# A change of TensorE's order inside the context loop of a Perceiver block: one run of sixteen 256-column matmuls a tile, in chunks 1 to 16

## The chip, the cores and the metric

The kernel runs on one core of a Trainium2 chip. The metric is the device time of one execution in microseconds (us). The kernel before took 857.74 us (median of three runs, 857.46 to 857.77).

## The reference, cut to what matters

128 latent tokens attend with linear attention to 12,544 context tokens of width 512 (16 heads of 32, 64 features a head); then come a second attention of cumulative sums and a router of two experts, which the change does not touch. Of the context the block needs

```python
k = heads(key, Wk, bk, Sk)                       # context @ Wk.T + bk
v = heads(value, Wv, bv, Sk)                     # context @ Wv.T + bv
k_prime = jax.nn.relu(jnp.einsum('bhnd,fd->bhnf', k, Wkf))
k_prime = k_prime * attention_mask[:, None, :, None]
kv = jnp.einsum('bhnf,bhne->bhfe', k_prime, v)   # summed over the tokens n
k_sum = jnp.sum(k_prime, axis=2)
```

## The kernel before, in words

**Precision.** Every operand of a large product is kept as two fp32r tensors: a high part (ScalarE's copy, rounded) and a low part (the rest, by a subtraction of VectorE or GpSimd). A full product is three matmuls, low x high, high x low and high x high (`three`, L808 to L812).

**Tiling.** The context comes in chunks of 512 tokens (24 of them, 0 to 23, and a last half chunk; `LAST` is 24), a chunk in four tiles of 128 tokens. For tile `n` = 4c + t TensorE does, in `period`:
- `values(n)`: jobs 0 and 1 of the features, then the tile's values into `v_bank`, 12 matmuls of 512 columns;
- `keys(c + 1, .., t)`: a quarter of the keys of the next chunk into `k_bank`, 12 matmuls of 512 columns, with jobs 2 and 3 behind the first three;
- `key_values(n - 1)`: features times values of the tile before, 8 matmuls of 256 columns, summed in `kv_ps` over the whole context.

A feature job (`feature_job`, L883) is two matmuls of 256 columns: keys of the tile by the high and low feature weights side by side. Jobs 0 and 2 go to the bank `f_ps[0]`, 1 and 3 to `f_ps[1]`. So in a tile there are two runs of 256-column matmuls, one of twelve (`key_values` and jobs 0, 1 of the next tile) and one of four (jobs 2, 3), and 24 matmuls of 512 columns.

**The other engines, in the order of their programs, for one tile:**
- ScalarE (`tile`, L589): the low half of jobs 0 and 1 out of the bank (`features_share`, L575: into the two-slot buffer `fb`), the high part of the features of the tile before (`features_high`, L581), the values' high part (L566), the high part of a context tile (`split_ctx_high`, L550), the shares of jobs 2 and 3, the keys' high part (`keys_high`, L558, two halves).
- VectorE (`tile`, L1316): sums of jobs 0, 1 (`features_sum`, L1287: bank plus `fb`, into `kf`), `features_low` of the tile before (L1300), the values' low part (L1278), sums of jobs 2, 3, relu and mask (`masked_features`, L1294), the keys' low part (`keys_low`, L1270, two halves).
- GpSimd (`period`, L464): the low part of a context tile (`split_ctx_low`, L453), then the features added to their running sum (`add_features`, L460), which waits for `kf_ready` (the mask).
- SyncE loads half a chunk of context at a time into the single buffer `ctx_raw`, when GpSimd has taken the low part of what was in it (L375, L376).

Each engine's queue is in order; semaphores with counts tie them. Work of chunks 17 to 21 on VectorE and ScalarE holds extra pieces besides (row sums, the split of later weights); in chunks 1 to 16 there are none.

Of the kernel before, what the change touches and what calls it, by code (L numbers as in the profile page):

```python
# [4 lines left out]
P = 128  # L5
D = 512
KC = D // P
# [6 lines left out]
CHUNK = 2 * HALF  # L14
TILES = CHUNK // P
NH_CTX = S_CTX // HALF
LAST = NH_CTX // 2
LAST_TILES = NH_CTX % 2 * (HALF // P)
NT = S_CTX // P
GRP = P // HD  # L20
GF = GRP * FD
# [2 lines left out]
JOBS = 4  # L24
# [38 lines left out]
def perceiver_kernel(nc, x_in, ctx_in, mask_in, wq_in, bq_in, wk_in, bk_in, wv_in, bv_in, bdq_in, bdk_in,  # L63
                     bo_in, wo_in, wr_in, stream_in, ident_in, tri_in, out):
    f32, f32r = mybir.dt.float32, mybir.dt.float32r
    ALU, ACT, AX = mybir.AluOpType, mybir.ActivationFunctionType, mybir.AxisListType

    ctx = ExitStack()
    with ctx:
# [146 lines left out]

        k_ps, v_ps = [k_bank[:, :], v_bank[:, :]], [kv_bank[1], kv_bank[2]]
        turn_ps = [kv_bank[3], f_ps[1]]
        o_ps = [v_bank, kv_bank[1]]
        val_ps = [kv_bank[1][:, 0:D // 2], kv_bank[2][:, 0:D // 2]]  # L220
        sum_ps = [f_ps[1][:, 0:D // 2], kv_bank[0][:, 0:D // 2]]
# [45 lines left out]
        ctx_lo_ready = sem("ctx_lo_ready")  # L267
# [3 lines left out]
        k_done = sem("k_done")  # L271
        k_hi_ready = sem("k_hi_ready")
        k_lo_ready = sem("k_lo_ready")
# [165 lines left out]
        def _(pool):  # L439
# [16 lines left out]
            def add_features(n, t, first=False):  # L456
# [4 lines left out]
                                   ksum_acc[:, :].rearrange("p (j f) -> p j f", f=P), kf[:, t % 2, :, :], ALU.add)\  # L461
                    .then_inc(ksum_added, 1)

            def period(c, s, splits=TILES):  # L464

                n = TILES * c
                for t in range(TILES):
                    if t < splits:
                        split_ctx_low(n + 2 * TILES + t, s, t)
                    add_features(n + t, t)  # L470
# [8 lines left out]
            for t in range(TILES):  # L479
                split_ctx_low(2 * TILES + t, 0, t)  # L480
                add_features(t, t, first=t == 0)
            with pool.Fori(1, LAST - 3, 2) as c:
                period(c, 1)
                period(c + 1, 0)
            period(LAST - 3, 1)
# [52 lines left out]
        def _(act):  # L538
# [47 lines left out]
                js = slice(b * NPAIR // 2, (b + 1) * NPAIR // 2)  # L586
                act.activation(kf_2[:, t, js, 0, :], kf[:, t, js, :], ACT.Copy).then_inc(kf_hi_ready, 1)

            def tile(n, t, first=False, keys=(), splits=()):  # L589

                for i in range(2):
                    features_share(n, i, first and t == 0)
                if not (first and t == 0):
                    features_high(n - 1, t - 1)
                values_high(n, t, first)
                for x in splits:

                    split_ctx_high(*x)
                features_share(n, 2, False)
                features_share(n, 3, False)  # L600
                for k in keys:
                    keys_high(*k)
# [24 lines left out]
            def period(c, s, splits=TILES, keys=CHUNK, pieces=0):  # L627
                n = TILES * c
                for t in range(TILES):
                    tile(n + t, t, keys=((c + 1, 1 - s, t, k_bank, keys),),  # L630
                         splits=((2 * c + 4 + t // 2, s, t),) if t < splits else ())
                    if pieces:
                        qkv_high(TILES * (pieces - 1) + t)

# [34 lines left out]
            with act.Fori(1, LAST - 5, 2) as c:  # L669
                period(c, 1)  # L670
                period(c + 1, 0)
            act.wait_ge(early_loaded, 16 * NPIECE)
            act.wait_ge(row_sums_ready, 2 * KC)
# [133 lines left out]
        def _(pe):  # L807
# [58 lines left out]
            def values_0(jobs):  # L866
# [13 lines left out]
                feature_job(*jobs[1])  # L880
                value_step(0, 0, 0, 3)

            def feature_job(c, s, n, t, i, first=False):  # L883

                if t == 0:

                    pe.wait_ge(k_lo_ready, 2 * (KC * c + i + 1))
                if not (first and t == 0 and i < 2):

                    pe.wait_ge(fsum_ready, JOBS * n + i - 1)  # L890
                for j in (2 * i, 2 * i + 1):
                    last = pe.matmul(f_ps[i % 2][:, (j % 2) * 2 * P:(j % 2 + 1) * 2 * P],  # L892
                                     keys_2[:, s, j, t * P:(t + 1) * P], bd[:, :, :].rearrange("p x f -> p (x f)"),
                                     start=True, stop=True)
                last.then_inc(f_done, 1)
# [35 lines left out]
                    if t > 0:  # L931
                        key_values(t - 1, t + 1, first=t == 1)

            def period(c, s, n_keys=CHUNK):
                n = TILES * c
                for t in range(TILES):
                    jobs = [(c, s, n + t, t, i) for i in range(JOBS)]
                    values(n + t, s, t, jobs[0:2])
                    keys(c + 1, 1 - s, t, jobs[2:4], n_keys)
                    key_values(n + t - 1, t + 1)  # L940

# [145 lines left out]
            pe.wait_ge(bd_lo_ready, 1)  # L1087

            period_0()
            with pe.Fori(1, LAST - 3, 2) as c:  # L1090
                period(c, 1)
                period(c + 1, 0)
            period(LAST - 3, 1)
            period(LAST - 2, 0)
            period(LAST - 1, 1, HALF)
            period_last(LAST, 0)
# [145 lines left out]
        def _(dve):  # L1242
# [48 lines left out]
            def masked_features(n, t):  # L1291

                dve.wait_ge(fsum_ready, JOBS * n + JOBS)
                dve.tensor_scalar(kf[:, t % 2, :, :], kf[:, t % 2, :, :], 0.0, mask[:, bass.ds(n, 1)], ALU.max,  # L1294
                                  ALU.mult)\
                   .then_inc(kf_ready, 1)

            def features_low(n, t):
                dve.wait_ge(kf_hi_ready, n + 1)
                dve.tensor_tensor(kf_2[:, t % 2, :, 1, :], kf[:, t % 2, :, :], kf_2[:, t % 2, :, 0, :].bitcast(f32),  # L1300
                                  ALU.subtract)\
                   .then_inc(kf_lo_ready, 1)
# [13 lines left out]
            def tile(n, t, first=False, keys=()):  # L1316

                features_sum(n, t, 0, first)
                features_sum(n, t, 1, False)
                if first and t == 0:  # L1320
                    queries_out()
                else:
# [46 lines left out]
            def period(c, s, keys=CHUNK, pieces=0, sums=None):  # L1369
                n = TILES * c  # L1370
                for t in range(TILES):
                    if sums is not None:
                        row_sum(sums, t)
                    i = TILES * (pieces - 1) + t
                    if pieces and i:
                        qkv_low(i - 1)
                    tile(n + t, t, keys=((c + 1, 1 - s, t, k_bank, keys),))

            def queries_out():
                for b in range(2):  # L1380
# [46 lines left out]
            with dve.Fori(1, LAST - 7, 2) as c:  # L1427
                period(c, 1)
                period(c + 1, 0)
            dve.wait_ge(sums_loaded, 16 * 2)  # L1430
            for i in range(2):
                period(LAST - 7 + i, 1 - i, sums=i)
# [220 lines left out]
```

## Time and profile before

| | |
|---|---|
| median of three runs | 857.74 us |
| the profiled execution | 857.43 us |
| its span | 855.5 us |
| TensorE, matmuls | 848.3 us busy, 99% of the span |
| VectorE | 678.6 us, 79% |
| ScalarE | 563.9 us, 66% |
| GpSimd | 375.0 us, 44% |
| granted TensorE clock | full in every slice |

The span is the time from the first to the last instruction of the profiled execution; the device time holds it and 1.9 us around it. Busy times of TensorE are those of pipelined matmuls whose recorded durations overlap; so it is the distance from one start to the next that tells its pace. Of the other engines two consecutive instructions can overlap by up to 0.1 us.

### The profile page before, as it was taken

What the parts mean: (1) busy time and instruction counts of PE and PEld (TensorE: products, weight loads), DVE (VectorE), ACT (ScalarE), POOL (GpSimd) and SP (SyncE); (2) the same over time, 40 slices, a digit from 0 to 9 for tenths busy, and PEclk for the clock granted to TensorE, in tenths of its full rate; (3) what the DMA queues carried; (4) which work ended last, traced back from release to release, by engine and by line L of the source; (5) the groups of instructions that cost most, each with busy time, mean ns of one, the idle gap of its engine ahead of it and who ended that gap; (6) DMA issues with size and microseconds to landing.
All of it is one profiled execution on the core that took longest, in us unless ns stands there. A gap on an engine that the chain in (4) does not pass through costs nothing.

```text
span 855.5 us, 14409 instructions
## 1 busy us (share of the span) xinstructions
PE 848.3 (99%) x4610; PEld 730.6 (85%) x4610; DVE 678.6 (79%) x1058; ACT 563.9 (66%) x1024; POOL 375.0 (44%) x221
## 2 busy tenths in 40 slices
PE   9999999999999999999999999999999999999998
PEld 7888888888888888888888888888888889878887
DVE  5777777777777777777777778888888878869997
ACT  5666666666666666666666666666777756677695
POOL 2555444545555444545555444544555433220210
PEclk9999999999999999999999999999999999999999
DMA  7212114010101001010101011010101000489840
GB/s 273 97 52 80 69 52 169 25 49 25 49 25 49 25 29 44 25 49 25 49 25 49 25 29 45 25 49 25 49 25 50 25 2 1 176 314 412 320 183 13
DMA packets 19529, 66.25 MB, mean 77 GB/s; under 512 B 2224, under 2 KB 2992, under 8 KB 19120
## 3 DMA queue, kind: packets, MB, share of 16 engines
q1 hardware_dynamic: 19072, 64.88, 20.6%
q10 hardware_dynamic: 432, 1.05, 0.3%
q8 instruction: 14, 0.23, 0.1%
q14 instruction: 11, 0.09, 0.0%
HBM read 65.66 MB, written 0.26 MB: 77 GB/s over the span
## 4 chain that ended last, share of the span: by engine, by line
PE 97%; DVE 1%; DMA 1%; ACT 0%; issue 0%; ACTq 0%; SPq 0%; DVEq 0%
PE side_ps L810 21%; PE side_ps L811 21%; PE side_ps L812 20%; PE kv_ps L905 11%; PE side_ps L892 11%; PE kv_ps L1191 4%; PE side_ps L1002 2%; PE side_ps L1008 2%; PE side_ps L1012 1%; DMA early<-in_wk 1%; PE side_ps L983 1%; PE kv_ps L1051 1%; PE kv_ps L1008 0%; PE kv_ps L1012 0%; PE kv_ps L1002 0%; PE side_ps L1084 0%
## 5 line engine op out<-in xcount | busy, mean ns | idle before, releaser
L460 POOL TENSOR_TENSOR ksum_acc<-ksum_acc,kf 128x1024 f32<-128x1024 f32 x97 | 233.0, 2402 | 86.9 <-DVE kf L1294 86.9
L453 POOL TENSOR_TENSOR ctx_lo<-ctx_raw,ctx_hi 128x512 fp32r<-128x512 f32 x92 | 119.2, 1296 | 273.8 <-ACT ctx_hi L550 273.8
L558 ACT ACTIVATE keys<-side_ps,bias_cols 64x512 fp32r<-64x512 f32 (+1 forms) x196 | 132.6, 677 | 148.9 <-PE side_ps L812 146.4
L1270 DVE SCALAR_TENSOR_TENSOR keys<-side_ps,bias_cols,keys 64x512 fp32r<-64x512 f32 (+1 forms) x196 | 144.8, 739 | 83.9 <-ACT keys L558 80.6
L1287 DVE TENSOR_TENSOR kf<-side_ps,fb 128x256 f32<-128x256 f32 x392 | 148.4, 420 | 16.6 <-ACT fb L575 5.2
L810 PE MATMUL side_ps<-wv_hi,ctx_lo 128*128 128x512 f32 x392 | 153.9, 393 | 0.0
L811 PE MATMUL side_ps<-wv_lo,ctx_hi 128*128 128x512 f32 x392 | 153.7, 392 | 0.0
L810 PE MATMUL side_ps<-ctx_hi,wk_lo 128*128 128x512 f32 (+1 forms) x400 | 153.6, 384 | 0.1
L811 PE MATMUL side_ps<-ctx_lo,wk_hi 128*128 128x512 f32 (+1 forms) x400 | 153.3, 383 | 0.0
L812 PE MATMUL side_ps<-wv_hi,ctx_hi 128*128 128x512 f32 x392 | 152.5, 389 | 0.0
L812 PE MATMUL side_ps<-ctx_hi,wk_hi 128*128 128x512 f32 (+1 forms) x400 | 152.2, 380 | 0.0
L575 ACT ACTIVATE fb<-side_ps 128x256 f32<-128x256 f32 x392 | 129.1, 382 | 8.5 <-PE side_ps L892 6.2
L1300 DVE TENSOR_TENSOR kf<-kf 128x1024 fp32r<-128x1024 f32 x96 | 118.3, 1233 | 12.5 <-ACT kf L581 12.5
L892 PE MATMUL side_ps<-bd,keys 128*128 128x256 f32 x784 | 126.5, 283 | 0.8 <-DVE kf L1287 0.8
L892 PEld LDWEIGHTS side_ps<-bd,keys 128*128 128x128 f32 x784 | 114.8, 190 | 9.3 <-DVE kf L1287 1.2
L566 ACT ACTIVATE v<-side_ps 128x512 fp32r<-128x512 f32 x98 | 58.7, 599 | 92.1 <-PE side_ps L812 92.1
L905 PEld LDWEIGHTS kv_ps<-kf,v 128*128 128x128 f32 x784 | 106.5, 190 | 7.6 <-issue 0.5
L905 PE MATMUL kv_ps<-kf,v 128*128 128x256 f32 x784 | 109.9, 283 | 0.3 <-DVE kf L1300 0.3
L581 ACT ACTIVATE kf<-kf 128x1024 fp32r<-128x1024 f32 x96 | 102.0, 1062 | 2.0
L1278 DVE TENSOR_TENSOR v<-side_ps,v 128x512 fp32r<-128x512 f32 x98 | 67.7, 690 | 29.8 <-ACT v L566 29.8
L812 PEld LDWEIGHTS side_ps<-ctx_hi,wk_hi 128*128 128x128 f32 x400 | 75.2, 188 | 15.1
L812 PEld LDWEIGHTS side_ps<-wv_hi,ctx_hi 128*128 128x128 f32 x392 | 73.6, 188 | 16.1
(203 smaller groups left out, 967.6 us busy)
## 6 DMA issues: line engine op xcount, KB each, us to landing
ctx_raw<-in_ctx SPq DMA_DIRECT2D x46, 512.0 KB, 3.2
early<-in_stream SPq DMA_DIRECT2D x15, 1024.0 KB, 8.3
raw<-in_stream SPq DMA_DIRECT2D x12, 1024.0 KB, 9.1
early<-in_stream SPq DMA_DIRECT2D x8, 512.0 KB, 4.1
early<-in_ctx SPq DMA_DIRECT2D x2, 512.0 KB, 6.0
early<-in_wv SPq DMA_DIRECT2D x1, 1024.0 KB, 7.7
early<-in_wq SPq DMA_DIRECT2D x1, 1024.0 KB, 9.2
early<-in_wo SPq DMA_DIRECT2D x1, 1024.0 KB, 7.0
```

The lines of the kernel that those rows point to most:

```text
L453: pool.tensor_tensor(ctx_lo[:, s, :, cols], raw[:, :, t % 2 * P:(t % 2 + 1) * P], ctx_hi[:, s, :, cols].bitcast(f32), ALU.subtract).then_i ...
L460: pool.tensor_tensor(ksum_acc[:, :].rearrange("p (j f) -> p j f", f=P), ksum_acc[:, :].rearrange("p (j f) -> p j f", f=P), kf[:, t % 2, :, ...
L558: act.activation(keys_2[rows, s, 2 * m + h, 0:n], src[rows, 0:n], ACT.Identity, bias=bias_cols[rows, KC + m:KC + m + 1]).then_inc(k_hi_rea ...
L575: act.activation(fb[:, i % 2, :, :], f_ps[i % 2][:, :].rearrange("p (j x f) -> p j x f", j=2, x=2) [:, :, 1, :], ACT.Copy).then_inc(fb_rea ...
L810: pe.matmul(out_ps, st_lo, mv_hi, start=start, stop=False, **kw)
L811: pe.matmul(out_ps, st_hi, mv_lo, start=False, stop=False, **kw)
L812: return pe.matmul(out_ps, st_hi, mv_hi, start=False, stop=stop, **kw)
L892: last = pe.matmul(f_ps[i % 2][:, (j % 2) * 2 * P:(j % 2 + 1) * 2 * P], keys_2[:, s, j, t * P:(t + 1) * P], bd[:, :, :].rearrange("p x f - ...
L905: return pe.matmul(kv_ps[:, j, :, :].rearrange("p x f -> p (x f)"), v_2[:, t % 2, j, :, :].rearrange("p x e -> p (x e)"), kf_2[:, t % 2, j ...
L1270: dve.scalar_tensor_tensor(out=keys_2[other, s, 2 * m + h, 0:n], in0=src[rows, 0:n], scalar=bias_cols[rows, KC + m:KC + m + 1], in1=keys_2 ...
L1287: dve.tensor_tensor(kf[:, t % 2, 2 * i:2 * i + 2, :], f_ps[i % 2][:, :].rearrange("p (j x f) -> p j x f", j=2, x=2)[:, :, 0, :], fb[:, i % ...
L1300: dve.tensor_tensor(kf_2[:, t % 2, :, 1, :], kf[:, t % 2, :, :], kf_2[:, t % 2, :, 0, :].bitcast(f32), ALU.subtract)\
```

## The change

In chunks 1 to 16 (`BURST` is 17) TensorE's order in a tile becomes: jobs 0 and 1, `key_values` of the tile before, jobs 2 and 3 (these are sixteen matmuls of 256 columns), the keys, the values of the **next** tile. The banks rotate: jobs 0 and 3 use `f_ps[0]`, jobs 1 and 2 share `f_ps[1]` and `k_bank` in turn, and the keys of a tile go to the bank of its job 1. So that the keys can follow at once, ScalarE takes all of job 1 out of its bank (a copy of the low half to `fb`, and one of the high half to `kf`), and VectorE's sum of job 1 is in SBUF, in place. ScalarE and VectorE make the high and low parts of the features in the same tile, behind the mask, and the keys' parts behind these. GpSimd waits for the mask with the context's low part, and for `features_low` (`kf_lo_ready`) with the addition. Chunk 17 is in the old order, without the values of its first tile (they were made at the end of chunk 16) and without the features of the tile before.

```diff
+BURST = LAST - 7
...
+        def burst_banks(t):
+            return [f_ps[0], k_bank, f_ps[1], f_ps[0]] if t % 2 else [f_ps[0], f_ps[1], k_bank, f_ps[0]]
...
         @block.gpsimd
+            def period_burst(c, s):
+                n = TILES * c
+                for t in range(TILES):
+                    pool.wait_ge(kf_ready, n + t + 1)
+                    split_ctx_low(n + 2 * TILES + t, s, t)
+                    pool.wait_ge(kf_lo_ready, n + t + 1)
+                    add_features(n + t, t)
...
         @block.scalar
+            def burst_share(n, t, i):
+                act.wait_ge(f_done, JOBS * n + i + 1)
+                act.wait_ge(fsum_ready, JOBS * n + i - 1)
+                both = burst_banks(t)[i].rearrange("p (j x f) -> p j x f", j=2, x=2)
+                last = act.activation(fb[:, i % 2, :, :], both[:, :, 1, :], ACT.Copy)
+                if i == 1:
+                    act.wait_ge(ksum_added, n - 1)
+                    act.wait_ge(kf_lo_ready, n - 1)
+                    last = act.activation(kf[:, t % 2, 2:4, :], both[:, :, 0, :], ACT.Copy)
+                last.then_inc(fb_ready, 1)
+
+            def tile_burst(n, t, keys, splits=()):
+                burst_share(n, t, 0)
+                burst_share(n, t, 1)
+                values_high(n, t, False)
+                burst_share(n, t, 2)
+                burst_share(n, t, 3)
+                for x in splits:
+                    split_ctx_high(*x)
+                features_high(n, t)
+                keys_high(*keys)
...
+            features_high(TILES - 1, TILES - 1)
+            with act.Fori(1, BURST, 2) as c:
+                period_burst(c, 1)
+                period_burst(c + 1, 0)
...
         @block.tensor
+            def burst_job(c, s, n, t, i):
+                if t == 0:
+                    pe.wait_ge(k_lo_ready, 2 * (KC * c + i + 1))
+                if i == 0:
+                    pe.wait_ge(fsum_ready, JOBS * n)
+                if i == 2:
+                    pe.wait_ge(k_lo_ready, 2 * (KC * (c + 1) + t))
+                if i == 3:
+                    pe.wait_ge(fsum_ready, JOBS * n + 1)
+                ps = burst_banks(t)[i]
...
+            def burst_keys(c, s, n, m):
+                pe.wait_ge(ctx_lo_ready, TILES * c)
+                pe.wait_ge(fb_ready, JOBS * n + 2)
+                for k in range(KC):
+                    last = three(burst_banks(m)[1], wk_hi[:, m, k, :], wk_lo[:, m, k, :],
+                                 ctx_hi[:, s, k, :], ctx_lo[:, s, k, :], k == 0, k == KC - 1)
...
+            def period_burst(c, s):
+                n = TILES * c
+                for t in range(TILES):
+                    for i in (0, 1):
+                        burst_job(c, s, n + t, t, i)
+                    key_values(n + t - 1, t + 1)
+                    for i in (2, 3):
+                        burst_job(c, s, n + t, t, i)
+                    burst_keys(c + 1, 1 - s, n + t, t)
+                    if t < TILES - 1:
+                        values(n + t + 1, s, t + 1, ())
+                    else:
+                        values(n + t + 1, 1 - s, 0, ())
...
-            with pe.Fori(1, LAST - 3, 2) as c:
-                period(c, 1)
-                period(c + 1, 0)
-            period(LAST - 3, 1)
+            values(TILES, 1, 0, ())
+            with pe.Fori(1, BURST, 2) as c:
+                period_burst(c, 1)
+                period_burst(c + 1, 0)
+            period(BURST, 1, behind_burst=True)
+            with pe.Fori(BURST + 1, LAST - 2, 2) as c:
+                period(c, 0)
+                period(c + 1, 1)
...
         @block.vector
+            def burst_sum(n, t, i):
...
+                dve.wait_ge(fb_ready, JOBS * n + i + 1)
+                sums = kf[:, t % 2, 2 * i:2 * i + 2, :]
+                high = burst_banks(t)[i].rearrange("p (j x f) -> p j x f", j=2, x=2)[:, :, 0, :]
+                dve.tensor_tensor(sums, sums if i == 1 else high, fb[:, i % 2, :, :], ALU.add).then_inc(fsum_ready, 1)
+
+            def tile_burst(n, t, keys):
+                burst_sum(n, t, 0)
+                burst_sum(n, t, 1)
+                values_low(n, t)
+                burst_sum(n, t, 2)
+                burst_sum(n, t, 3)
+                masked_features(n, t)
+                features_low(n, t)
+                keys_low(*keys)
```

## Rows read from the trace of the kernel before

**Rows 1.** Page: span, then busy us (share) and instructions of each engine.

```profile
span 855.5 us, 14409 instructions
PE 848.3 (99%) x4610; PEld 730.6 (85%) x4610; DVE 678.6 (79%) x1058; ACT 563.9 (66%) x1024; POOL 375.0 (44%) x221
```

**Rows 2.** Page: shares of the chain that ended last, by engine.

```profile
PE 97%; DVE 1%; DMA 1%; ACT 0%; issue 0%; ACTq 0%; SPq 0%; DVEq 0%
```

**Rows 3.** Stretches: us, busy us (instructions) of PE, PEld, DVE, ACT, POOL, clock, DMA, GB/s.

```profile
53.00:485.00 432.00, 432.00 (x2340) 374.80 (x2339) 331.37 (x525) 278.17 (x527) 216.85 (x117) 1.00 0.14 49
```

**Rows 4.** Waits of TensorE, whole span: us in total, times, longest.

```profile
PE side_ps L892 <- DVE kf L1287: 0.8, 1, 0.8
```

**Rows 5.** Timeline of TensorE, one tile: start us, us, then the group and its count.

```profile
305.01 1.11 PE L905 MATMUL kv_ps<-kf,v 128*128 128x256 f32 x8
305.96 0.64 PE L892 MATMUL side_ps<-bd,keys 128*128 128x256 f32 x4
306.44 0.40 PE L810 MATMUL side_ps<-wv_hi,ctx_lo 128*128 128x512 f32 x1
...
307.61 0.39 PE L812 MATMUL side_ps<-wv_hi,ctx_hi 128*128 128x512 f32 x1
...
309.87 0.64 PE L892 MATMUL side_ps<-bd,keys 128*128 128x256 f32 x4
310.34 0.40 PE L810 MATMUL side_ps<-ctx_hi,wk_lo 128*128 128x512 f32 x1
...
312.41 0.28 PE L905 MATMUL kv_ps<-kf,v 128*128 128x256 f32 x1
```

**Rows 6.** Groups by shape, 60 to 480 us: busy us, mean ns | idle before.

```profile
L1270 DVE SCALAR_TENSOR_TENSOR keys<-side_ps,bias_cols,keys 64x512 fp32r<-64x512 f32 x114 | 85.4, 750 | 49.7 <-ACT keys L558 47.9
...
L575 ACT ACTIVATE fb<-side_ps 128x256 f32<-128x256 f32 x226 | 74.1, 382 | 1.4
...
L1300 DVE TENSOR_TENSOR kf<-kf 128x1024 fp32r<-128x1024 f32 x57 | 69.8, 1225 | 9.3 <-ACT kf L581 9.3
...
L581 ACT ACTIVATE kf<-kf 128x1024 fp32r<-128x1024 f32 x57 | 60.6, 1063 | 1.4
...
L566 ACT ACTIVATE v<-side_ps 128x512 fp32r<-128x512 f32 x57 | 34.1, 598 | 58.8 <-PE side_ps L812 58.8
```

**Rows 7.** Timeline, all engines, at 709 us.

```profile
709.14 0.64 PE L892 MATMUL side_ps<-bd,keys 128*128 128x256 f32 x4
...
709.58 0.66 ACT L575 ACTIVATE fb<-side_ps 128x256 f32<-128x256 f32 x2
```

**Rows 8.** Timeline of VectorE at 710 us.

```profile
709.62 0.69 DVE L1278 TENSOR_TENSOR v<-side_ps,v 128x512 fp32r<-128x512 f32 x1 [0.39 <-ACT v L566]
710.23 0.75 DVE L1287 TENSOR_TENSOR kf<-side_ps,fb 128x256 f32<-128x256 f32 x2
```

**Rows 9.** Timeline of VectorE at 311 us.

```profile
310.81 0.76 DVE L1287 TENSOR_TENSOR kf<-side_ps,fb 128x256 f32<-128x256 f32 x2
311.70 0.75 DVE L1294 TENSOR_SCALAR kf<-kf,mask 128x1024 f32<-128x1024 f32 x1
```

**Rows 10.** Timeline of GpSimd at 311 us.

```profile
310.59 1.29 POOL L453 TENSOR_TENSOR ctx_lo<-ctx_raw,ctx_hi 128x512 fp32r<-128x512 f32 x1 [3.06 <-ACT ctx_hi L550]
312.53 2.40 POOL L460 TENSOR_TENSOR ksum_acc<-ksum_acc,kf 128x1024 f32<-128x1024 f32 x1 [0.65 <-DVE kf L1294]
```

**Rows 11.** Timelines of GpSimd and VectorE in the last full chunk.

```profile
711.85 2.41 POOL L460 TENSOR_TENSOR ksum_acc<-ksum_acc,kf 128x1024 f32<-128x1024 f32 x1 [4.90 <-DVE kf L1294]
...
713.88 1.46 DVE L1300 TENSOR_TENSOR kf<-kf 128x1024 fp32r<-128x1024 f32 x1 [0.30 <-ACT kf L581]
```

**Rows 12.** Timeline, all engines, at 740 us: VectorE releases a weight load.

```profile
739.43 0.68 DVE L1307 TENSOR_TENSOR kf<-kf 128x512 fp32r<-128x512 f32 x1
...
740.17 0.30 PEld L905 LDWEIGHTS kv_ps<-kf,v 128*128 128x128 f32 x2
```

**Rows 13.** Page: DMA issues: times, KB each, median us from issue to landing.

```profile
ctx_raw<-in_ctx SPq DMA_DIRECT2D x46, 512.0 KB, 3.2
```

More of the change, by code:

```diff
@@ L481, in _ @@
                 add_features(t, t, first=t == 0)
-            with pool.Fori(1, LAST - 3, 2) as c:
+            with pool.Fori(1, BURST, 2) as c:
+                period_burst(c, 1)
+                period_burst(c + 1, 0)
+            with pool.Fori(BURST, LAST - 3, 2) as c:
                 period(c, 1)
@@ L587, in features_high_half, with tile @@
                 act.activation(kf_2[:, t, js, 0, :], kf[:, t, js, :], ACT.Copy).then_inc(kf_hi_ready, 1)
-            def tile(n, t, first=False, keys=(), splits=()):
+            def burst_share(n, t, i):
[18 more added lines that the diff above has]
+                keys_high(*keys)
+            def tile(n, t, first=False, keys=(), splits=(), former=True):
                 for i in range(2):
                     features_share(n, i, first and t == 0)
-                if not (first and t == 0):
+                if former and not (first and t == 0):
                     features_high(n - 1, t - 1)
@@ L625, in qkv_high, with period @@
                 act.activation(high(g)[:, k, :], raw(g)[:, k, :], ACT.Copy).then_inc(qkv_hi_ready, 1)
-            def period(c, s, splits=TILES, keys=CHUNK, pieces=0):
+            def period_burst(c, s):
+                n = TILES * c
+                for t in range(TILES):
+                    tile_burst(n + t, t, (c + 1, 1 - s, t, burst_banks(t)[1], CHUNK),
+                               splits=((2 * c + 4 + t // 2, s, t),))
+            def period(c, s, splits=TILES, keys=CHUNK, pieces=0, behind_burst=False):
                 n = TILES * c
@@ L630, in period @@
                     tile(n + t, t, keys=((c + 1, 1 - s, t, k_bank, keys),),
-                         splits=((2 * c + 4 + t // 2, s, t),) if t < splits else ())
+                         splits=((2 * c + 4 + t // 2, s, t),) if t < splits else (),
+                         former=t > 0 or not behind_burst)
                     if pieces:
@@ L668, in _ @@
                 tile(t, t, first=t < 2, keys=((1, 1, t, k_bank, CHUNK),), splits=((4 + t // 2, 0, t),))
-            with act.Fori(1, LAST - 5, 2) as c:
-                period(c, 1)
+            features_high(TILES - 1, TILES - 1)
+            with act.Fori(1, BURST, 2) as c:
+                period_burst(c, 1)
+                period_burst(c + 1, 0)
+            for c in range(BURST, LAST - 5, 2):
+                period(c, 1, behind_burst=c == BURST)
                 period(c + 1, 0)
@@ L881, in values_0 @@
                 value_step(0, 0, 0, 3)
+            def burst_job(c, s, n, t, i):
[8 more added lines that the diff above has]
+                ps = burst_banks(t)[i]
+                for j in (2 * i, 2 * i + 1):
+                    last = pe.matmul(ps[:, (j % 2) * 2 * P:(j % 2 + 1) * 2 * P],
+                                     keys_2[:, s, j, t * P:(t + 1) * P], bd[:, :, :].rearrange("p x f -> p (x f)"),
+                                     start=True, stop=True)
+                last.then_inc(f_done, 1)
+            def burst_keys(c, s, n, m):
[4 more added lines that the diff above has]
+                                 ctx_hi[:, s, k, :], ctx_lo[:, s, k, :], k == 0, k == KC - 1)
+                last.then_inc(k_done, 1)
             def feature_job(c, s, n, t, i, first=False):
@@ L932, in period_0, with period_burst, period @@
                         key_values(t - 1, t + 1, first=t == 1)
-            def period(c, s, n_keys=CHUNK):
+            def period_burst(c, s):
+                n = TILES * c
+                for t in range(TILES):
+                    for i in (0, 1):
[8 more added lines that the diff above has]
+                        values(n + t + 1, 1 - s, 0, ())
+            def period(c, s, n_keys=CHUNK, behind_burst=False):
                 n = TILES * c
@@ L937, in period @@
                     jobs = [(c, s, n + t, t, i) for i in range(JOBS)]
-                    values(n + t, s, t, jobs[0:2])
+                    if t == 0 and behind_burst:
+                        pe.wait_ge(fsum_ready, JOBS * n)
+                        for job in jobs[0:2]:
+                            feature_job(*job)
+                    else:
+                        values(n + t, s, t, jobs[0:2])
                     keys(c + 1, 1 - s, t, jobs[2:4], n_keys)
@@ L1089, in _ @@
             period_0()
-            with pe.Fori(1, LAST - 3, 2) as c:
-                period(c, 1)
-                period(c + 1, 0)
-            period(LAST - 3, 1)
+            values(TILES, 1, 0, ())
+            with pe.Fori(1, BURST, 2) as c:
+                period_burst(c, 1)
+                period_burst(c + 1, 0)
+            period(BURST, 1, behind_burst=True)
+            with pe.Fori(BURST + 1, LAST - 2, 2) as c:
+                period(c, 0)
+                period(c + 1, 1)
             period(LAST - 2, 0)
@@ L1314, in masked_features_last, with tile @@
                    .then_inc(kf_ready, 1)
-            def tile(n, t, first=False, keys=()):
+            def burst_sum(n, t, i):
+                if i == 0:
+                    dve.wait_ge(ksum_added, n - 1)
+                    dve.wait_ge(kf_lo_ready, n - 1)
+                dve.wait_ge(fb_ready, JOBS * n + i + 1)
[11 more added lines that the diff above has]
+                keys_low(*keys)
+            def tile(n, t, first=False, keys=(), former=True):
                 features_sum(n, t, 0, first)
@@ L1321, in tile @@
                     queries_out()
-                else:
+                elif former:
                     features_low(n - 1, t - 1)
@@ L1367, in row_sum, with period_burst, period @@
                    .then_inc(row_sums_ready, 1)
-            def period(c, s, keys=CHUNK, pieces=0, sums=None):
+            def period_burst(c, s):
+                n = TILES * c
+                for t in range(TILES):
+                    tile_burst(n + t, t, (c + 1, 1 - s, t, burst_banks(t)[1], CHUNK))
+            def period(c, s, keys=CHUNK, pieces=0, sums=None, behind_burst=False):
                 n = TILES * c
@@ L1376, in period @@
                         qkv_low(i - 1)
-                    tile(n + t, t, keys=((c + 1, 1 - s, t, k_bank, keys),))
+                    tile(n + t, t, keys=((c + 1, 1 - s, t, k_bank, keys),), former=t > 0 or not behind_burst)
             def queries_out():
@@ L1426, in _ @@
                 tile(t, t, first=t < 2, keys=((1, 1, t, k_bank, CHUNK),))
-            with dve.Fori(1, LAST - 7, 2) as c:
-                period(c, 1)
-                period(c + 1, 0)
+            features_low(TILES - 1, TILES - 1)
+            with dve.Fori(1, BURST, 2) as c:
+                period_burst(c, 1)
+                period_burst(c + 1, 0)
             dve.wait_ge(sums_loaded, 16 * 2)
             for i in range(2):
-                period(LAST - 7 + i, 1 - i, sums=i)
+                period(LAST - 7 + i, 1 - i, sums=i, behind_burst=i == 0)
             period(LAST - 5, 1, pieces=1)
```

## The prediction, made before the changed kernel ran

> **What bounds the kernel now.** I read the page first. TensorE is busy for 848.3 of the 855.5 us of the span, VectorE for 79% of it [rows 1], and the chain that ended last is TensorE for 97% [rows 2]. A busy TensorE may still stand at waits, so the next view is the stretch of steady tiles, 53 to 485 us: TensorE 432.00 of 432.00 us, at the full clock [rows 3], and among its waits the longest one on VectorE in the loop's code is 0.8 us, once in the whole span [rows 4]. So TensorE's own stream is the limit, and only its length, or a new wait in it, can move the time.
>
> The timeline of one tile shows what the stream costs [rows 5]. A tile is 312.41 - 305.01 = 7.40 us. The run of twelve 256-column matmuls takes 306.44 - 305.01 = 1.43 (0.12 each), the run of four 309.87 to 310.34 = 0.47. Ten 512-column matmuls later in a row take 309.87 - 307.61 = 2.26, 0.226 each; but the first five behind a run take 307.61 - 306.44 = 1.17, where 1.13 would be due. So each change from 256 to 512 columns costs some 0.03 to 0.04, and the start of a run gives 0.01 back (1.43 for twelve, 0.47 for four). The whole tile says the same: 7.40 - 16 x 0.12 - 24 x 0.226 = 0.06, over two runs 0.03 each; with 0.227 for 0.226 (rounding) it is 0.02. I take 0.02 a run, bounds 0.015 to 0.035.
>
> **The change, part by part.**
>
> *TensorE's work.* No matmul is added or removed. One run of sixteen stands where there were two: 0.02 saved in each of 16 x 4 = 64 tiles, -1.3 us (bounds -1.0 and -2.2). A tile would be 7.38. A run of sixteen isn't in the trace; the runs of four and twelve cost the same, so I take that for sixteen too.
>
> *The new order's waits.* I count from the start of job 0, T = 0. TensorE's starts: job 1 0.23, `key_values` 0.47, job 2 1.43, job 3 1.67, keys 1.91, values of the next tile 4.66, next tile 7.38. A weight load starts with the matmul before its own, so a wait costs nothing if it is over by 1.31 (job 2), 1.55 (job 3), 1.79 (keys).
>
> ScalarE can start on job 0 0.44 after T (709.58 - 709.14) and takes the second share 0.28 later [rows 7]: with 0.38 each [rows 6] job 0's share ends at 0.82, job 1's at 1.10. The added copy of job 1's high half has the shape of L575, so 0.38 (bounds 0.28, two in a row less their overlap, and 0.43 with a gap), and ends at 1.4 to 1.5. The keys wait for it: 0.06 from an engine's end to the weight load (739.43 + 0.68 to 740.17) [rows 12], 1.56 against 1.79. Hidden, cover 0.2. The values' high part, 0.60 [rows 6], ends at 1.9 to 2.12.
>
> VectorE's low part of the values starts at V = 1.9 to 2.15. From there the features are one chain: 0.61 to the next sum (710.23 - 709.62), 0.75 for two sums [rows 8], 0.13 and 0.75 for the mask (310.81 + 0.76 = 311.57, then 311.70) [rows 9]: mask done at V + 2.24. It releases ScalarE's high part (1.06 [rows 6], with 0.06 around it done at V + 3.36) and GpSimd's low part of the context 0.08 later (311.70 + 0.75 = 312.45, then 312.53), 1.29 long [rows 10]: V + 3.61.
>
> *GpSimd against VectorE.* `features_low` reads two SBUF tensors. Alone it takes 1.225 [rows 6]; in the last full chunk it started 0.38 before GpSimd's addition ended, took 1.46, and ended 713.88 + 1.46 = 715.34, that is 1.08 after GpSimd's end at 714.26 [rows 11]: it had stood still until then. In the new order it would start at V + 3.36 with GpSimd busy until V + 3.61, so it ends at F = V + 3.61 + 1.08 = V + 4.69, instead of V + 4.59. Behind it GpSimd adds: 0.08 + 2.40 [rows 10], until F + 2.48. VectorE meanwhile does the two low halves of the keys, 0.75 each [rows 6] with 0.03 between, until F + 1.56, and the sum of job 0 (0.42), until F + 2.0. Then comes the sum of job 1, which is now in SBUF with two SBUF inputs: it stands still until F + 2.48 and ends 0.29 later (a quarter of the 1.08, and 0.02; bounds 0.27, and 0.42 for the whole sum). The next V is F + 2.77 - 0.08 = F + 2.69.
>
> So there is a loop through VectorE, ScalarE's shadow and GpSimd that TensorE isn't in: 4.69 + 2.69 = **7.38** a tile, against TensorE's 7.38. Through TensorE: the sum of job 0 ends at F + 2.0, job 3's load may be 0.06 later, and must be there by 7.38 + 1.55: F up to 6.87, V up to 2.18; V is 1.9 to 2.15. The keys' low parts (F + 1.62 against 7.38 + 1.31) have 0.5 to spare. A stall isn't forced, but the cover is 0.03 to 0.28, and 0.01 too much in the loop costs 0.64 us over 64 tiles, once that cover is gone. I take 0.1 us in all.
>
> The Trainium skill states it as a rule, page "SBUF — State Buffer", section "SBUF: two separate sides": the port pair that VectorE and GpSimd share is an exclusive lock, held for the whole instruction by whoever starts first, and a VectorE instruction with two SBUF inputs takes part in it against a GpSimd one that reads SBUF. The trace agrees with its 1.46 for 1.23. Without such a lock the sum of job 1 would end at F + 2.4, and the loop would be 7.38 - 0.37 - 0.10 = 6.9, clear of TensorE's tile.
>
> *Context load.* SyncE issues it behind GpSimd's low part of an odd tile, at 5.5 to 5.8; 3.2 to landing [rows 13] makes 9.1 with 0.2 for the issue; ScalarE wants it at 7.38 + 2.4 = 9.8, and isn't on the chain until 7.38 + V + 2.24 - 0.62 = 11. Hidden, cover 0.7 and 1.9.
>
> *Into the loop.* TensorE makes the values of tile 4, then jobs 0, 1, then `key_values` of tile 3: 0.96 + 2.75 + 0.35 = 4.06 behind the last keys. `features_low` of tile 3 now stands behind the keys' parts: with 0.75 as bound for ScalarE's halves too, 0.2 + 1.5 + 1.06 + 1.23 = 4.0. Nothing, up to 0.3, once.
>
> *Out of the loop.* Chunk 17 has only jobs 0, 1 between the values made early and its first keys, and these go to `k_bank`, where the keys of tile 67 lie until F + 1.56. The load could be at 7.38 + 0.35 = 7.73; with F = 6.6 to 6.84 it is at 8.2 to 8.45. Cost 0.5 to 0.7 once, I take 0.6. Nothing hides it.
>
> **Sum.** -1.3 + 0.1 + 0 + 0.6 = -0.6. On the profiled execution, 857.43 (855.5 of span and 1.9 around it) becomes 856.8; that execution lies 0.3 under the median of the runs, 857.74, so the forecast is 857.1, 0.07% down.
>
> **The rivals.**
>
> *The loop of the shared port is longer than TensorE's tile* (slower). The place: the sum of job 1 behind `add_features`, and `features_low` behind the context's low part. For it: the two lengths are equal within my rounding, of thirteen terms each good to 0.01 or so; and two terms use the overlap of 0.08 between VectorE instructions of which I have seen only one of the pairs. Against it: every term is a measured row, and where they didn't overlap they'd cost 0.11 each. Price: 64 x (L - 7.38) less the cover. L = 7.44 gives 857.1 + 3.6 = 860.7; L = 7.60 (no overlap) 871. It decides from L = 7.42 on, where 2.3 us are lost and the kernel is over 0.2% slower.
>
> *A run costs 0.035, and both seams are free* (faster). -2.2, so 855.5. For it: the 1.17 for five matmuls in rows 5. Against it: the bank at the way out must be free, and the tile's sum leaves 0.06 for both runs at most.
>
> *The change doesn't do what it says*: what I lay to the change of width belongs to something in both orders (a price per matmul), a tile stays 7.40, and the seam is left: 858.4. Against it: the extra stands in the first five matmuls behind each run and not later.
>
> *The context comes late*: a load of over 5.1 us instead of 3.2 holds ScalarE's high part; each us over it is 1 us every second tile, 32 us in all. No load of this size is near it.
>
> **How the numbers follow.** Less than 0.2%, 1.7 us, can't be told from no change here. Forecast 0.58, and the change without effect 0.08, both within: 0.66, and of the first rival its mild part 0.02, together 0.68. Slower: the rest of the first rival 0.25, the context 0.02: 0.27. Faster: 0.05. The range goes down to 856.3 (a run at 0.03, no stall but the seam) and up to 862.0 (L = 7.46); above it lies 0.12, below 0.04. The likeliest case alone is 856.4 to 858.2.
>
> **What would show it.** Tiles of 7.38 from one `key_values` run to the next in chunks 1 to 16, and 7.40 behind them; the in-place sum at 0.5 to 0.8 instead of 0.42, ending 0.29 behind GpSimd's addition; `features_low` at 1.3 to 1.35, ending 1.08 behind the context's low part; one wait of TensorE of 0.5 to 0.7 on the keys' low part of tile 67. Wrong it would be if job 3 waited for VectorE in every tile, with tiles longer than 7.40; or if the in-place sum took 0.42 beside GpSimd's addition.

## The result, and the profile after

The changed kernel takes 863.43 us (median of six runs, 863.28 to 863.75) against 857.68 us for the kernel before (857.41 to 857.77): ratio 1.0066, 95% interval 1.0056 to 1.0076. It is 5.75 us slower; the forecast was 857.1, with a range up to 862.0. The forecast named the cause as its first rival, and gave it 0.27 (0.25 for a slower kernel, 0.02 for a stall too small to tell).

The page, the stretch of steady tiles, and the chain by engine, of the changed kernel; they answer to [rows 1 to 3]:

```profile
span 861.6 us, 14473 instructions
PE 853.4 (99%) x4610; PEld 734.6 (85%) x4610; DVE 704.8 (82%) x1058; ACT 584.1 (68%) x1088; POOL 375.0 (44%) x221
PE 96%; DVE 1%; DMA 1%; ACT 0%; issue 0%; ACTq 0%; SPq 0%; DVEq 0%
53.00:485.00 432.00, 432.00 (x2322) 374.93 (x2321) 351.65 (x520) 293.16 (x578) 213.58 (x116) 1.00 0.14 48
```

These views show almost nothing, and that is the first thing to see. TensorE counts as busy for 432.00 of 432.00 us as before, but with 2322 matmuls in them instead of 2340. A matmul that is held for less than 0.1 us is recorded as a longer one (in the tile below a group of four takes 0.70 instead of 0.64), and no wait is listed. What tells is the distance between starts, and the busy time of the others: VectorE is busy for 351.65 us instead of 331.37.

TensorE's timeline of one tile (start us, us, group and count), to be laid beside [rows 5]:

```profile
303.92 0.64 PE L952 MATMUL side_ps<-bd,keys 128*128 128x256 f32 x4
304.39 1.12 PE L989 MATMUL kv_ps<-kf,v 128*128 128x256 f32 x8
305.35 0.70 PE L952 MATMUL side_ps<-bd,keys 128*128 128x256 f32 x4
305.88 0.39 PE L863 MATMUL side_ps<-ctx_hi,wk_lo 128*128 128x512 f32 x1
...
311.35 0.64 PE L952 MATMUL side_ps<-bd,keys 128*128 128x256 f32 x4
```

The tile is 311.35 - 303.92 = 7.43. Jobs 2 and 3 took 0.70 where jobs 0 and 1 took 0.64: job 3 waited for VectorE. From one run of `key_values` to the next, the first three burst tiles are 7.380, as forecast; then they vary from 7.42 to 7.61, with one of 7.81. The 63 of them from 58.09 to 528.17 us take 470.08, 7.462 each, against TensorE's own 7.38 and the 7.400 of before.

VectorE and GpSimd in the same tile, against [rows 8 to 11]:

```profile
302.06 1.41 DVE L1408 TENSOR_TENSOR kf<-kf 128x1024 fp32r<-128x1024 f32 x1 [1.13 <-ACT kf L598]
303.50 1.53 DVE L1378 SCALAR_TENSOR_TENSOR keys<-side_ps,bias_cols,keys 64x512 fp32r<-64x512 f32 x2
305.06 0.42 DVE L1432 TENSOR_TENSOR kf<-side_ps,fb 128x256 f32<-128x256 f32 x1
305.41 0.83 DVE L1432 TENSOR_TENSOR kf<-kf,fb 128x256 f32<-128x256 f32 x1
306.16 0.68 DVE L1386 TENSOR_TENSOR v<-side_ps,v 128x512 fp32r<-128x512 f32 x1
306.76 0.74 DVE L1432 TENSOR_TENSOR kf<-side_ps,fb 128x256 f32<-128x256 f32 x2
307.63 0.75 DVE L1402 TENSOR_SCALAR kf<-kf,mask 128x1024 f32<-128x1024 f32 x1
309.51 1.41 DVE L1408 TENSOR_TENSOR kf<-kf 128x1024 fp32r<-128x1024 f32 x1 [1.13 <-ACT kf L598]
```

```profile
303.55 2.40 POOL L465 TENSOR_TENSOR ksum_acc<-ksum_acc,kf 128x1024 f32<-128x1024 f32 x1 [1.16 <-DVE kf L1408]
308.54 1.29 POOL L458 TENSOR_TENSOR ctx_lo<-ctx_raw,ctx_hi 128x512 fp32r<-128x512 f32 x1 [2.59 <-DVE kf L1402]
311.00 2.41 POOL L465 TENSOR_TENSOR ksum_acc<-ksum_acc,kf 128x1024 f32<-128x1024 f32 x1 [1.16 <-DVE kf L1408]
```

Read in a circle, this is the loop of the forecast. `features_low` ends at 303.47, and GpSimd adds the features from 303.55 to 305.95. The in-place sum of job 1 starts at 305.41, stands still, and ends at 306.24, 0.28 behind GpSimd in the mean. Values and two sums follow without a gap, and the mask ends at 308.38. Then GpSimd takes the context's low part, but at 308.54, 0.16 behind the mask and not 0.08, until 309.83; `features_low` starts at 309.51, stands, and ends at 310.92, 1.08 behind it. From addition to addition it is 311.00 - 303.55 = 7.45. The parts measured over the tiles give the same sum: 0.16 + 1.29 + 1.08 to the end of `features_low`, 0.08 + 2.41 + 0.28 to the end of the in-place sum, 1.39 to the mask's start and 0.75 for the mask, 7.44.

### The profile page after: what moved, and what is told of

The parts are those of the page before. It is cut to its first block, busy times and chain, and to the rows that moved or that the text cites. A ratio compares the mean times of both kernels' runs of the same rounds, so it can differ in the third digit from the quotient of the medians.

```text
span 861.6 us, 14473 instructions
## 1 busy us (share of the span) xinstructions
PE 853.4 (99%) x4610; PEld 734.6 (85%) x4610; DVE 704.8 (82%) x1058; ACT 584.1 (68%) x1088; POOL 375.0 (44%) x221
## 4 chain that ended last, share of the span: by engine, by line
PE 96%; DVE 1%; DMA 1%; ACT 0%; issue 0%; ACTq 0%; SPq 0%; DVEq 0%
PE side_ps L863 20%; PE side_ps L864 20%; PE side_ps L865 20%; PE kv_ps L989 11%; PE side_ps L952 8%; PE side_ps L976 4%; PE kv_ps L1299 4%; PE side_ps L1106 2%; PE side_ps L1112 2%; PE side_ps L1116 1%; DMA early<-in_wk 1%; PE side_ps L1087 1%; PE kv_ps L1155 1%; PE kv_ps L1112 0%; PE kv_ps L1116 0%; PE kv_ps L1106 0%
## 5 line engine op out<-in xcount | busy, mean ns | idle before, releaser
L1408 DVE TENSOR_TENSOR kf<-kf 128x1024 fp32r<-128x1024 f32 x96 | 129.9, 1354 | 74.5 <-ACT kf L598 74.3
L611 ACT ACTIVATE fb<-side_ps 128x256 f32<-128x256 f32 x256 | 91.3, 383 | 82.0 <-PE side_ps L952 70.0
L989 PEld LDWEIGHTS kv_ps<-kf,v 128*128 128x128 f32 x784 | 102.7, 191 | 2.6 <-issue 0.5
L952 PE MATMUL side_ps<-bd,keys 128*128 128x256 f32 x512 | 87.5, 292 | 0.0
L863 PEld LDWEIGHTS side_ps<-ctx_hi,wk_lo 128*128 128x128 f32 x400 | 75.5, 189 | 13.1 <-issue 1.4
L863 PEld LDWEIGHTS side_ps<-wv_hi,ctx_lo 128*128 128x128 f32 x392 | 73.7, 188 | 14.0
L864 PEld LDWEIGHTS side_ps<-ctx_lo,wk_hi 128*128 128x128 f32 x400 | 75.5, 189 | 11.7 <-issue 0.5
L864 PEld LDWEIGHTS side_ps<-wv_lo,ctx_hi 128*128 128x128 f32 x392 | 73.7, 188 | 13.7
```

The source lines that it names most:

```text
L611: last = act.activation(fb[:, i % 2, :, :], both[:, :, 1, :], ACT.Copy)
L863: pe.matmul(out_ps, st_lo, mv_hi, start=start, stop=False, **kw)
L864: pe.matmul(out_ps, st_hi, mv_lo, start=False, stop=False, **kw)
L952: last = pe.matmul(ps[:, (j % 2) * 2 * P:(j % 2 + 1) * 2 * P], keys_2[:, s, j, t * P:(t + 1) * P], bd[:, :, :].rearrange("p x f -> p (x f) ...
L989: return pe.matmul(kv_ps[:, j, :, :].rearrange("p x f -> p (x f)"), v_2[:, t % 2, j, :, :].rearrange("p x e -> p (x e)"), kf_2[:, t % 2, j ...
```

## The experiments

Every ratio is against the kernel before on the same chip, where its medians were 857.72 to 857.85. A difference to the changed kernel compares medians of two chips and is good to some 0.2 us.

**GpSimd's addition made small.**

`part` is the number of blocks of 128 features that are added, of 8:

```diff
-                    add_features(n + t, t)
+                    add_features(n + t, t, part=1)
```

> In chunks 1 to 16 GpSimd adds only the first 128 of the 1024 features to the running sum (the rest of the key sums of these chunks is left out), so its addition is about 0.4 us instead of 2.40. Theory (a loop through the shared port: features_low, addition, in-place sum of job 1 held until the addition ends, mask, context's low part, features_low): the in-place sum no longer waits (0.42 instead of 0.83), the loop falls to about 7.1, under TensorE's tile, tiles are 7.38, the kernel 863.4 - 64 x 0.08 = 858.3 us. Rival (the chain of VectorE and ScalarE through job 3 alone holds TensorE, the port waits only fill its slack): tiles stay 7.46, 863.4 us.

Measured 858.02 us (ratio 1.0002, 0.9993 to 1.0011). GpSimd, then VectorE:

```profile
300.68 0.46 POOL L466 TENSOR_TENSOR ksum_acc<-ksum_acc,kf 128x128 f32<-128x128 f32 x1 [1.16 <-DVE kf L1408]
```

```profile
302.20 0.43 DVE L1432 TENSOR_TENSOR kf<-side_ps,fb 128x256 f32<-128x256 f32 x1
302.72 0.43 DVE L1432 TENSOR_TENSOR kf<-kf,fb 128x256 f32<-128x256 f32 x1
```

The in-place sum takes 0.43 when GpSimd's addition is over, and 61 of the burst tiles are 7.380. VectorE's and ScalarE's programs are unchanged, so the rival falls: their chain alone does not hold TensorE.

**The addition made longer.**

```diff
+                    pool.wait_ge(ksum_added, n + t)
                     pool.wait_ge(kf_lo_ready, n + t + 1)
+                    pool.tensor_tensor(ksum_acc[:, 0:P], ksum_acc[:, 0:P], kf[:, t % 2, 0, :], ALU.add)\
+                        .then_inc(same_again, 1)
+                    pool.wait_ge(same_again, n + t - TILES + 1)
                     add_features(n + t, t)
```

> The changed kernel with GpSimd's addition made longer: in chunks 1 to 16 it adds the first 128 of the 1024 features once more in front of the whole addition (their key sums are then counted twice), 0.46 us and a wait of some 0.05 between. Port loop: every tile longer by all of it, 7.46 + 0.51 = 7.97, 863.4 + 64 x 0.51 = 896 us. Rival (job 3 alone, or a plain shortage of VectorE's time): GpSimd is only 44% busy and no tile changes, 863.4 us.

Measured 902.04 us (median of two runs; ratio 1.0517, 1.0498 to 1.0536). GpSimd, then VectorE's `features_low` in front of it and the in-place sum behind it:

```profile
306.68 0.46 POOL L478 TENSOR_TENSOR ksum_acc<-ksum_acc,kf 128x128 f32<-128x128 f32 x1 [1.23 <-DVE kf L1413]
307.23 2.39 POOL L466 TENSOR_TENSOR ksum_acc<-ksum_acc,kf 128x1024 f32<-128x1024 f32 x1
```

```profile
305.13 1.41 DVE L1413 TENSOR_TENSOR kf<-kf 128x1024 fp32r<-128x1024 f32 x1 [1.13 <-ACT kf L603]
...
308.47 1.42 DVE L1437 TENSOR_TENSOR kf<-kf,fb 128x256 f32<-128x256 f32 x1
```

The kernel is 38.6 us longer than the changed one, 0.60 for each of 64 tiles. GpSimd, which is busy for only 44% of the changed kernel's span, sets the time, one for one. The forecast of 896 was 6 too low, 0.09 a tile, and the trace places it. The whole addition starts 307.23 - 306.68 = 0.55 behind the small one (0.54 in the mean, 0.51 forecast). The small one starts 0.145 behind the end of `features_low` in most tiles, 0.16 in the mean, where the changed kernel's addition starts 0.08 behind it. Together the addition starts 0.62 later, and it takes 0.02 less. In the trace the wait for `features_low` is here a semaphore instruction of its own in front of the small addition; in the changed kernel the addition carries it itself.

**GpSimd's waits in the other order.**

```diff
-                    pool.wait_ge(kf_ready, n + t + 1)
-                    split_ctx_low(n + 2 * TILES + t, s, t)
+                    split_ctx_low(n + 2 * TILES + t, s, t, behind=n + t + 1)
...
                 pool.wait_ge(ctx_hi_ready, g - TILES + 1)
+                if behind is not None:
+                    pool.wait_ge(kf_ready, behind)
```

> The changed kernel, but GpSimd waits for ctx_hi_ready first and for the mask (kf_ready) directly in front of the context's low part, so that the register instruction for the other wait's count is no longer behind the mask. Theory of the port loop: context's low part 0.08 instead of 0.16 behind the mask, loop 7.46 - 0.08 = 7.38, level with TensorE: 863.4 - 5.1 = 858.3 us, up to 859.5 if the one tile in eight with a longer mask start still sticks out. Rival (job 3 alone): GpSimd's start doesn't matter, 863.4 us.

Measured 858.63 us (ratio 1.0010, 1.0001 to 1.0019), 4.8 under the changed kernel. VectorE, then GpSimd:

```profile
302.98 0.76 DVE L1433 TENSOR_TENSOR kf<-kf,fb 128x256 f32<-128x256 f32 x1
...
305.14 0.75 DVE L1403 TENSOR_SCALAR kf<-kf,mask 128x1024 f32<-128x1024 f32 x1
307.02 1.32 DVE L1409 TENSOR_TENSOR kf<-kf 128x1024 fp32r<-128x1024 f32 x1 [1.13 <-ACT kf L599]
```

```profile
305.97 1.29 POOL L460 TENSOR_TENSOR ctx_lo<-ctx_raw,ctx_hi 128x512 fp32r<-128x512 f32 x1 [2.50 <-DVE kf L1403]
```

The mask ends at 305.89 and GpSimd starts at 305.97, 0.08 behind. The in-place sum is still held (0.76), but the loop is now level with TensorE: 54 tiles are 7.380. This is the largest part of the loss, in one pair of swapped waits. In the trace of the changed kernel the wait for the mask sits on a register instruction, the one that works out the count for the next wait: it is recorded 0.04 behind the mask's end, and GpSimd's low part starts 0.12 behind it. With the waits swapped the low part carries the wait for the mask itself.

The order in the source does not decide this alone. In the kernel with the longer addition the wait that blocks stands last, directly in front of the small addition, and is still compiled into an instruction of its own (0.145 instead of 0.08); in the changed kernel two more waits with computed counts stand behind the wait for `features_low` in `add_features`, and the addition starts at 0.08.

**Job 1's sum from its bank.**

```diff
-                if i == 1:
-
-                    act.wait_ge(ksum_added, n - 1)
-                    act.wait_ge(kf_lo_ready, n - 1)
-                    last = act.activation(kf[:, t % 2, 2:4, :], both[:, :, 0, :], ACT.Copy)
...
-                pe.wait_ge(fb_ready, JOBS * n + 2)
+                pe.wait_ge(fsum_ready, JOBS * n + 2)
...
-                dve.tensor_tensor(sums, sums if i == 1 else high, fb[:, i % 2, :, :], ALU.add).then_inc(fsum_ready, 1)
+                dve.tensor_tensor(sums, high, fb[:, i % 2, :, :], ALU.add).then_inc(fsum_ready, 1)
```

> The changed kernel, but job 1's sum reads its high half from the bank (one SBUF input, no copy by ScalarE), and TensorE's keys wait for that sum instead of ScalarE's share. Theory of the port loop: this sum is not held by GpSimd's addition, 0.41 instead of 0.83; the chain through TensorE is V = 1.65, F = V + 4.77 = 6.4, the sum of job 1 ends at 1.65 of the tile against 1.79: tiles 7.38, 858.3 us less a shorter stall at the way out, 858.0. Rival (job 3 alone): TensorE gets one more wait on VectorE at the keys, tiles 7.46 or more, 863.4 us or above.

Measured 857.63 us (ratio 0.9997, 0.9989 to 1.0006). VectorE's sums of jobs 0 and 1, and GpSimd's addition, which runs until 302.72:

```profile
302.08 0.76 DVE L1426 TENSOR_TENSOR kf<-side_ps,fb 128x256 f32<-128x256 f32 x2 [0.28 <-ACT fb L611]
```

```profile
300.32 2.40 POOL L465 TENSOR_TENSOR ksum_acc<-ksum_acc,kf 128x1024 f32<-128x1024 f32 x1 [1.16 <-DVE kf L1402]
```

Two sums in 0.76 beside a running addition: with one SBUF input the sum isn't held, and VectorE even waits 0.28 for ScalarE. The edit also takes ScalarE's copy of job 1 away, so it changes two things; the small addition above changes GpSimd's alone. 62 tiles are 7.380, with GpSimd's start still 0.16 behind the mask: the order of its waits matters only while the loop is closed.

**The way out of the burst order, TensorE's side.**

```diff
-                    else:
+                    elif not last:
                         values(n + t + 1, 1 - s, 0, ())
...
-            period(BURST, 1, behind_burst=True)
+            period_burst(BURST - 2, 1)
+            period_burst(BURST - 1, 0, last=True)
+            pe.wait_ge(fsum_ready, JOBS * TILES * BURST)
+            period(BURST, 1)
```

> The changed kernel with another way out of the burst order: TensorE's last burst tile (tile 67) leaves the values of tile 68 to chunk 17, which then begins in the old order, jobs 0 and 1 and the values in front of the first keys. The 64 burst tiles stay as they are (7.46). If the two waits at the way out (0.7 on the keys' low part, 1.0 on the sum of job 0 behind a row sum) are all that the seam costs, -1.7 us: 861.7. If they are given back later in chunk 17, where VectorE has the row sums, 863.4.

Measured 863.33 us (ratio 1.0065, 1.0051 to 1.0079): nothing gained, where 861.7 was expected. In the changed kernel the way out, TensorE and then VectorE, is

```profile
535.28 0.63 PE L976 MATMUL side_ps<-bd,keys 128*128 128x256 f32 x4
536.57 0.47 PE L863 MATMUL side_ps<-ctx_hi,wk_lo 128*128 128x512 f32 x1 [0.65 <-DVE keys L1378]
...
537.74 0.81 PE L976 MATMUL side_ps<-bd,keys 128*128 128x256 f32 x4 [0.24 <-DVE kf L1395]
```

```profile
534.89 1.53 DVE L1378 SCALAR_TENSOR_TENSOR keys<-side_ps,bias_cols,keys 64x512 fp32r<-64x512 f32 x2
536.45 0.69 DVE L1495 TENSOR_REDUCE row_sums<-early 128x1 f32<-128x512 f32 x1
537.17 0.76 DVE L1395 TENSOR_TENSOR kf<-side_ps,fb 128x256 f32<-128x256 f32 x2
```

and without the early values TensorE comes to the same keys at the same time:

```profile
536.60 0.47 PE L863 MATMUL side_ps<-ctx_hi,wk_lo 128*128 128x512 f32 x1 [0.62 <-DVE keys L1381]
```

The values of tile 68 stand in front of these keys in either order, so TensorE's work up to them is the same; what it waits for is VectorE's queue: the keys' low part, a row sum of 0.69, then the sum of job 0, for which job 2 stands. The expectation's wait of 1.0 for job 2 was misread: a wait of that length is in the trace at 32 us, and at tile 68 only 0.24 is listed. From start to start more is seen. The keys start 536.57 - 535.28 = 1.29 behind four matmuls of 0.47, so TensorE stood for 0.82; job 2 starts 1.17 behind the keys' first matmul.

**The row sum behind the sums.**

```diff
-            def tile(n, t, first=False, keys=(), former=True):
+            def tile(n, t, first=False, keys=(), former=True, between=()):
...
                 features_sum(n, t, 1, False)
+                for i in between:
+                    row_sum(i, t)
...
-                    if sums is not None:
+                    late = behind_burst and t == 0
+                    if sums is not None and not late:
                         row_sum(sums, t)
...
+                    tile(n + t, t, keys=((c + 1, 1 - s, t, k_bank, keys),), former=t > 0 or not behind_burst,
+                         between=(sums,) if late else ())
```

> The changed kernel with nothing but the row sum of chunk 17's first tile moved behind the sums of jobs 0 and 1. The wait of 1.0 us of job 2 of tile 68 should shrink by 0.69, the one of 0.7 on the keys' low part stay: 862.7 us. If the row sum isn't on the path, 863.4.

Measured 862.82 us (ratio 1.0061, 1.0047 to 1.0074), 0.6 under the changed kernel. TensorE:

```profile
536.46 0.47 PE L863 MATMUL side_ps<-ctx_hi,wk_lo 128*128 128x512 f32 x1 [0.63 <-DVE keys L1378]
...
537.23 0.64 PE L976 MATMUL side_ps<-bd,keys 128*128 128x256 f32 x4
```

Job 2 now starts 0.77 behind the keys' first matmul instead of 1.17, and the four matmuls take 0.64 instead of 0.81: this stall is gone. The interval of the way out is 11.67 instead of 12.29.

**The edits together.** Sum of job 1 from its bank, with the new way out, with and without the order of GpSimd's waits, and then with the row sum moved as well:

> The changed kernel with the sum of job 1 from its bank, GpSimd's waits in the other order, and the new way out, all three. The loop of the shared port is open (its sum isn't held), the tiles are TensorE's 7.38, and the seam has no wait: 64 x 0.02 = 1.3 us under the kernel before, 856.4; if the way in or out still holds a wait, 856.4 to 857.2.

> As the kernel with all three edits, but GpSimd's waits as in the changed kernel. If the order of the waits matters only while the loop of the shared port is closed, the same as with it: 856.4 us, tiles 7.38. If the 0.08 sits on TensorE's path also without the in-place sum, tiles 7.40 or more and 857.7 or above.

> The kernel with all three edits (sum of job 1 from its bank, GpSimd's waits in the other order, new way out), and in chunk 17's first tile VectorE's row sum (0.69) behind the sums of jobs 0 and 1 instead of in front of them. In the trace without it TensorE's job 2 of tile 68 stands until VectorE has done the keys' low part, the row sum and the sum of job 0; if that is the rest of the seam, -0.7 to -0.85: 856.6 us, and the 66 tiles from 2 to 68 take 487.2 us instead of 488.0. If the stall is given back elsewhere, 857.4.

Measured: with the order of the waits 857.39 us (0.9995, 0.9986 to 1.0004), without it 857.44 (0.9999, 0.9990 to 1.0008), so the order of the waits adds nothing once the loop is open. Both miss the 856.4 of the expectations by 1.0. With the order of the waits the burst tiles are TensorE's own, but the two intervals at the way in and out take 15.66 where two tiles of 7.40 are 14.80, so it was the seam that was not free. With the row sum moved 856.82 us against 857.84 (ratio 0.9988, 0.9979 to 0.9997): under both kernels, and under the kernel before by 1.0 us (by its interval 0.3 to 1.8) of the 1.3 that 64 tiles of 0.02 are worth; the two intervals of the seam still take 15.09. The tiles' sum over the 66 from tile 2 to 68 is 487.48 us; 488.40 before, 493.94 in the changed kernel.

**The price of a run, in the kernel before.**

```diff
-                    keys(c + 1, 1 - s, t, jobs[2:4], n_keys)
+                    keys(c + 1, 1 - s, t, jobs[2:4], n_keys, apart=True)
```

> The kernel before, with job 3 behind the ninth matmul of the keys instead of next to job 2: three runs of 256-column matmuls a tile (twelve, two, two) in chunks 1 to 23, no matmul more. If a change from 256 to 512 columns costs 0.02: tiles 7.42, 92 x 0.02 = +1.8 us, 859.5. If the price belongs to the matmuls and not to the change: 857.7.

Measured 858.66 us (ratio 1.0009, 1.0000 to 1.0017), where 859.5 was expected.

```profile
303.15 0.40 PE L892 MATMUL side_ps<-bd,keys 128*128 128x256 f32 x2
...
304.77 0.40 PE L892 MATMUL side_ps<-bd,keys 128*128 128x256 f32 x2
...
305.70 1.11 PE L905 MATMUL kv_ps<-kf,v 128*128 128x256 f32 x8
306.65 0.64 PE L892 MATMUL side_ps<-bd,keys 128*128 128x256 f32 x4
...
310.56 0.40 PE L892 MATMUL side_ps<-bd,keys 128*128 128x256 f32 x2
```

Tiles of 310.56 - 303.15 = 7.41 (7.407 in the mean). Two runs of two in place of one of four cost 0.007, a third of what I gave a run: the price is not the same for every run. What the tiles measure are differences: a run of four and one of twelve cost 0.020 more than one of sixteen (7.400 against 7.380). If each of these is put at 0.02, an assumption that fits, a run of two comes to 0.0135.

## Why the prediction was wrong

*TensorE's own tile* was right: 7.380, one run fewer worth 0.02, -1.3 us in all, seen where nothing held it.

*The step that failed is the loop of the shared port, put at **7.38** a tile "against TensorE's 7.38", and with it "I take 0.1 us in all".* The mechanism was right term by term: addition 2.40, held sum 0.28 behind it (0.29 forecast), 1.08 behind the context's low part, the overlaps of 0.08. One term was mis-sized: "GpSimd's low part of the context 0.08 later". I took the 0.08 from a GpSimd instruction that carries its blocking wait itself [rows 9, 10]. In the diff a second wait with a computed count stands behind the blocking one, and the trace shows the blocking one on a register instruction in front; 0.16 is what it measured. Swapping the two gave back 4.8 of the 5.75 us. A second one is small: the mask starts 0.24 behind the sum in one tile of eight, at the end of the loop's body, and not 0.13; that is 0.015 a tile in the mean, and makes the intervals of GpSimd's additions 7.56 to 7.58 there (once it starts 0.49 behind, which is the tile of 7.81). Together 63 tiles cost 470.08 - 63 x 7.38 = 5.1 us.

The loop had been worked out as just as long as TensorE's tile, from terms rounded to 0.01, and "0.01 too much in the loop costs 0.64 us" stood beside it. To call no stall the likeliest case was then a choice of the cheap side, and the 0.27 for the rival didn't follow from the sum. The price of the rival was right: for a loop of 7.46 the prediction gives 862.0, and the 1.1 us more of the way out make it 863.1, against 863.43.

*The way out* was 1.66 us (the tiles from 53.92 to 58.09 and from 528.17 to 540.46 take 16.46, where two of 7.40 are 14.80), not 0.6. The wait on the keys' low part was forecast at 0.5 to 0.7; 0.65 is listed, and 0.82 is what it takes from start to start. A second stall, that of job 2, was not in the chain at all: the row sum of chunk 17 stands in front of the sum of job 0. It had been named among the kernel's extra work. Moving it gave 0.6. The remaining 0.2 or so is not placed.

*The way in, the context load, ScalarE's copy* were hidden as forecast.

The sum with the measured sizes: -1.3 + 5.1 + 1.7 = +5.5, of 5.75.

## What to carry to other kernels

When an order is rewritten so that one engine's instructions are locked out by another's, add up the loop that goes through both, in hundredths, and compare it with the bound engine's period. If they are equal, give the stall at least the weight of the free case: here the two terms that were too small both made the loop longer. In a loop with computed counts look in the trace at how far the guarded instruction starts behind its releaser. Putting the wait that will block last can save 0.08, as it did here, but only if the compiled instruction then carries that wait itself. And a TensorE that is 100% busy in the profile may still be waiting: measure from start to start.

## What the runs showed of the hardware

A GpSimd instruction that carries its blocking wait itself starts 0.08 us after the releasing VectorE instruction; it starts 0.16 after it when the wait sits on a register instruction in front, and 0.145 in most tiles when the wait is a semaphore instruction of its own. A VectorE addition of 256 columns takes 0.42 to 0.43 us with one SBUF input beside a GpSimd addition or with two when GpSimd rests, and with two beside it ends 0.28 after GpSimd's end. Two runs of two 256-column matmuls cost TensorE 0.007 us more than one of four, and runs of four and twelve 0.020 more than one of sixteen. A VectorE subtraction of 1024 columns with two SBUF inputs ends 1.08 behind the end of the GpSimd instruction that holds it.
